# A two-layer graph attention network with a feed-forward block: how the second softmax fetches its 2 x 10,000 logits

## What is computed

```python
as_n = jnp.einsum('nhd,hd->nh', h, a_src)
ad_n = jnp.einsum('nhd,hd->nh', h, a_dst)
e = jax.nn.leaky_relu(as_n[src] + ad_n[dst], NEG_SLOPE)
e_max = jax.lax.stop_gradient(jax.ops.segment_max(e, dst, num_segments=N))
ex = jnp.exp(e - e_max[dst])
denom = jax.ops.segment_sum(ex, dst, num_segments=N)
alpha = ex / (denom[dst] + 1e-16)
```

## Time and profile before

| | |
|---|---|
| median of 3 runs | 4287.79 us (4287.08 to 4290.51) |
| time of the profiled execution | 4294.91 us |
| its span, first to last instruction | 4293.2 us |
| PE busy | 3523.8 us (82%) |
| POOL busy | 1009.2 us (24%) |
| second softmax, first clearing to the store of its records | 3483.73 to 3715.99 us |

### The profile page before, as it was taken

The page is one execution under the profiler, slowest core; times in us unless marked ns, Lnnn a source line. Parts: engine busy times, 40 slices in busy tenths (PEclk is TensorE's granted clock), DMA queues, the critical chain, the costliest instruction groups (busy, mean ns, idle before and its releaser), DMA issues. The chain is left out here.

```text
span 4293.2 us, 67317 instructions
## 1 busy us (share of the span) xinstructions
PE 3523.8 (82%) x21804; PEld 2146.3 (50%) x21805; DVE 2163.2 (50%) x5213; ACT 1302.1 (30%) x2233; POOL 1009.2 (24%) x1392
## 2 busy tenths in 40 slices
PE   4850039999999999999999999999999930188898
PEld 3640025566555655565556555655565520055565
DVE  8877254434443444334434443344334300389998
ACT  2531113322332233223322332233223300044444
POOL 2448710000000000000000000000000037466665
PEclk9985559999999999999999999999999975599999
DMA  8862011111111111111121111111111000278887
GB/s 256 256 211 61 3 38 40 44 56 34 48 40 56 37 46 37 57 38 45 38 56 38 46 40 53 39 48 38 53 39 48 29 13 1 49 213 231 231 230 211
DMA packets 147427, 337.78 MB, mean 79 GB/s; under 512 B 81880, under 2 KB 81880, under 8 KB 139738
## 3 DMA queue, kind: packets, MB, share of 16 engines
q1 hardware_dynamic: 111883, 240.88, 18.4%
q0 software_dynamic: 34112, 93.04, 8.5%
q10 hardware_dynamic: 1175, 0.05, 0.0%
HBM read 266.09 MB, written 124.25 MB: 91 GB/s over the span
## 5 line engine op out<-in xcount | busy, mean ns | idle before, releaser
L942 POOL DMA_INDIRECT lay_rows<-parts,lay_idx x200 | 210.1, 1051 | 2536.2 <-PE lay_pz L1185 1619.2
L1219 PE MATMUL lay_pm<-lay_zh,w1h 128*128 128x500 f16 x1920 | 718.4, 374 | 25.3 <-DVE lay_h L1105 20.1
L1220 PE MATMUL lay_pm<-lay_zl,w1h 128*128 128x500 f16 x1920 | 718.6, 374 | 1.8 <-issue 1.3
L1221 PE MATMUL lay_pm<-lay_zh,w1l 128*128 128x500 f16 x1920 | 718.4, 374 | 0.0
L1026 DVE SCALAR_TENSOR_TENSOR lay_zl<-lay_pz,lay_zh 128x400 f16<-128x400 f32 x600 | 320.4, 574 | 710.7 <-ACT lay_zh L1136 710.5
L1136 ACT ACTIVATE lay_zh<-lay_pz 128x400 f16<-128x400 f32 x600 | 298.3, 504 | 1056.9 <-PE lay_pz L1185 1053.2
L1145 ACT ACTIVATE lay_ex<-lay_pm,b1c,scale 128x500 f32<-128x500 f32 x320 | 245.6, 768 | 869.8 <-PE lay_pm L1221 869.8
L1243 PE MATMUL lay_pm<-w2h,lay_gh 128*128 128x512 f16 x1280 | 484.9, 379 | 0.0
L1243 PE MATMUL lay_pm<-w2h,lay_gl 128*128 128x512 f16 x1280 | 483.9, 378 | 0.0
L1243 PE MATMUL lay_pm<-w2l,lay_gh 128*128 128x512 f16 x1280 | 483.4, 378 | 0.0
L1061 DVE TENSOR_SCALAR lay_ex<-lay_ex,scale 128x500 f32<-128x500 f32 x320 | 153.7, 480 | 568.0 <-ACT lay_ex L1145 568.0
(11 more groups left out here) (278 smaller groups left out, 5775.1 us busy)
## 6 DMA issues: line engine op xcount, KB each, us to landing
x<-in_x_dram SPq DMA_DIRECT2D x20, 1500.0 KB
out_x<-x SPq DMA_DIRECT2D x100, 288.0 KB
out_own<-h SPq DMA_DIRECT2D x100, 288.0 KB
out_dram<-out_x SPq DMA_DIRECT2D x100, 288.0 KB
nrm_xb<-in_x_dram SPq DMA_DIRECT2D x20, 1344.0 KB
parts<-nrm_parts SPq DMA_DIRECT2D x20, 1344.0 KB
h<-lay_h SPq DMA_DIRECT2D x80, 336.0 KB
nrm_w<-in_L_gnn_W_dram SPq DMA_DIRECT2D x6, 1024.0 KB, 19.3
```

Of the source, the lines that this page charges most:

```text
L1219: pe.matmul(o, c.w1h[:, d, cols], zh[:, d, h], start=(d == 0), stop=False)
L1220: pe.matmul(o, c.w1h[:, d, cols], zl[:, d, h], start=False, stop=False)
L1221: ins = pe.matmul(o, c.w1l[:, d, cols], zh[:, d, h], start=False, stop=(d == DC - 1))
```

## The change

The second softmax looks its logits up on chip; the first one stays as it was. A node number is split into its low 7 bits and its high part (0 to 78). The table of 10,000 pairs is loaded once into SBUF as `nodes` (two transfers of SP, from the same `logit2`) and turned by two PE transposes into `tab`: 128 partitions (the low part) by 2 x 79 (the high part). The low parts of the edges are turned the same way into `low_t`.

The 79 columns of edges are worked off in items: 20 items of up to 4 columns for the sources (one value wanted), 27 items of up to 3 columns for the destinations (two values wanted), 47 in all. For an item i of n columns

- *spread* on PE: n f32 matmuls, weights 79 x 128 (a column of the identity, repeated), 128 columns of `low_t` streamed: each of 128 partitions gets a copy of the 128 low parts;
- *apart* on ACT: absolute value of (low part - partition number), 128 x 128n, from PSUM;
- *one* on ACT: relu(1 - that), the one-hot matrix, 128 x 128n;
- *look* on PE: n f32 matmuls, weights 128 x 128 (the one-hot matrix), 79 or 158 columns of `tab` streamed: for each edge the row of the table that has its low part;
- *pick* on DVE: n operations of 128 x 79 or 128 x 158 from PSUM, which keep the entry with the right high part and set the others to zero, and one reduction, which adds them up into `gsrc` or `gdst`.

Tiles between the engines have two buffers. The 158 indirect transfers of this stage are gone; POOL only makes two small ramps (`iota`). What comes behind L685 is unchanged.

```diff
+LOWS = 128
+HIGHS = -(-N // LOWS)
...
+    SIDES = (("src", 1, 4), ("dst", 2, 3))
...
+        self.items = [(side, at, min(group, EC - at)) for side, (_, _, group) in enumerate(self.SIDES)
+                      for at in range(0, EC, group)]
...
+        self.spread = [m.ps(f"spread{b}", [LOWS, 4, EP]) for b in range(2)]
+        self.rows = [m.ps(f"rows{b}", [EP, 512]) for b in range(2)]
...
+    def sync(self, sp):
+        whole, rest = N // LOWS, N % LOWS
+        sp.wait_ge(self.nodes_free, 1)
+        sp.dma_start(self.nodes[0:whole], self.table[0:whole * LOWS, :].rearrange("(p l) h -> p (l h)", l=LOWS))\
+            .then_inc(self.nodes_in, 16)
+        sp.dma_start(self.nodes[whole:whole + 1, 0:rest], self.table[whole * LOWS:N, :].rearrange("(p l) h -> p (l h)", p=1))\
+            .then_inc(self.nodes_in, 16)
+
+    def first(self, dve):
+        self.nc.vector.memset(self.nodes[:], 0.0).then_inc(self.nodes_free, 1)
...
+    def vector(self, dve, ch):
+        nc = self.nc
+        for side, index in enumerate(self.index):
+            ch.put(nc.vector.tensor_scalar(self.cut[:, side, 0], index[:], LOWS - 1, None, ALU.bitwise_and))
+            ch.put(nc.vector.tensor_scalar(self.cut[:, side, 1], index[:], 7, None, ALU.logical_shift_right))
+        ch.wait()
+        nc.vector.tensor_copy(self.cutf[:], self.cut[:]).then_inc(self.cut_ready, 1)
+        dve.wait_ge(self.placed, 2)
+        nc.vector.tensor_copy(self.minus[:], self.place[:]).then_inc(self.highs_ready, 1)
+        ch.put(nc.vector.tensor_copy(self.highs[:], self.highi[:]))
+        dve.wait_ge(self.cut_ready, 1)
+        ch.wait()
+        dve.wait_ge(self.lows_turned, 1)
+        nc.vector.tensor_copy(self.low_t[:], self.spread[0][0:EC, 0:2]).then_inc(self.lows_ready, 1)
+        dve.wait_ge(self.tab_turned, 1)
+        nc.vector.tensor_copy(self.tab[:], self.rows[0][:, 0:2 * HIGHS].rearrange("p (v h) -> p v h", v=2))\
+            .then_inc(self.tab_ready, 1)
+
+        def add(i):
+            side, at, n = self.items[i]
+            values = self.SIDES[side][1]
+            dve.wait_ge(self.picked_ready, i + 1)
+            nc.vector.tensor_reduce(self.found[side][:, at:at + n, 0:values],
+                                    self.picked[:, i % 2, 0:n * values].rearrange("p (c v) h -> p c v h", v=values),
+                                    AX.X, ALU.add).then_inc(self.sums, 1)
+
+        for i, (side, at, n) in enumerate(self.items):
+            values = self.SIDES[side][1]
+            dve.wait_ge(self.rows_done, i + 1)
+            if i >= 2:
+                dve.wait_ge(self.sums, i - 1)
+            for k in range(n):
+                ins = nc.vector.scalar_tensor_tensor(
+                    out=self.picked[:, i % 2, k * values:k * values + values],
+                    in0=self.highs[:].rearrange("p (a h) -> p a h", a=1).broadcast_to([EP, values, HIGHS]),
+                    scalar=self.cutf[:, side, 1, at + k:at + k + 1],
+                    in1=self.rows[i % 2][:, k * values * HIGHS:(k + 1) * values * HIGHS].rearrange("p (v h) -> p v h", h=HIGHS),
+                    op0=ALU.is_equal, op1=ALU.mult)
+            ins.then_inc(self.picked_ready, 1)
+            if i:
+                add(i - 1)
+        add(len(self.items) - 1)
+        dve.wait_ge(self.sums, len(self.items))
+
+    def scalar(self, act):
+        nc = self.nc
+        act.wait_ge(self.highs_ready, 1)
+
+        def one_hot(i):
+            n = self.items[i][2]
+            act.wait_ge(self.apart_ready, i + 1)
+            if i >= 2:
+                act.wait_ge(self.rows_done, i - 1)
+            nc.scalar.activation(self.one[:, i % 2, 0:n], self.apart[:, i % 2, 0:n], ACT.Relu, bias=1.0, scale=-1.0)\
+                .then_inc(self.one_ready, 1)
+
+        for i, (_, _, n) in enumerate(self.items):
+            act.wait_ge(self.spread_done, i + 1)
+            if i >= 2:
+                act.wait_ge(self.one_ready, i - 1)
+            nc.scalar.activation(self.apart[:, i % 2, 0:n], self.spread[i % 2][:, 0:n], ACT.Abs, bias=self.minus[:])\
+                .then_inc(self.apart_ready, 1)
+            if i:
+                one_hot(i - 1)
+        one_hot(len(self.items) - 1)
+
+    def tensor(self, pe):
+        c = self.c
+        pe.wait_ge(self.cut_ready, 1)
+        for side in range(2):
+            ins = pe.transpose(self.spread[0][0:EC, side], self.cutf[:, side, 0], c.ident[0:EP, 0:EP])
+        ins.then_inc(self.lows_turned, 1)
+        pe.wait_ge(self.nodes_in, 32)
+        for v in range(2):
+            ins = pe.transpose(self.rows[0][:, v * HIGHS:v * HIGHS + HIGHS], self.nodes[:, :, v], c.ident[0:HIGHS, 0:HIGHS])
+        ins.then_inc(self.tab_turned, 1)
+        pe.wait_ge(self.lows_ready, 1)
+        pe.wait_ge(self.tab_ready, 1)
+
+        def look(i):
+            side, at, n = self.items[i]
+            width = self.SIDES[side][1] * HIGHS
+            pe.wait_ge(self.one_ready, i + 1)
+            if i >= 2:
+                pe.wait_ge(self.picked_ready, i - 1)
+            for k in range(n):
+                ins = pe.matmul(self.rows[i % 2][:, k * width:k * width + width], self.one[:, i % 2, k],
+                                self.tab[:, 0:self.SIDES[side][1]].rearrange("p v h -> p (v h)"), start=True, stop=True)
+            ins.then_inc(self.rows_done, 1)
+
+        for i, (side, at, n) in enumerate(self.items):
+            if i >= 2:
+                pe.wait_ge(self.apart_ready, i - 1)
+            for k in range(n):
+                ins = pe.matmul(self.spread[i % 2][:, k], c.ident[0:EC, at + k:at + k + 1].broadcast_to([EC, LOWS]),
+                                self.low_t[:, side], start=True, stop=True)
+            ins.then_inc(self.spread_done, 1)
+            if i:
+                look(i - 1)
+        look(len(self.items) - 1)
...
@@ -647,6 +802,9 @@
         def _(pool):
             if more:
                 more.gpsimd(pool)
+            if match:
+                match.gpsimd(pool)
+                return
             pool.wait_ge(loaded, 16 * 9)
             for idx, out, sem in ((src, gsrc, got_src), (dst, gdst, got_dst)):
                 for k in range(EC):
@@ -677,8 +837,11 @@
             ch.put(nc.vector.tensor_scalar(cont[:], first[:], -1.0, 1.0, ALU.mult, ALU.add))
             if more:
                 more.vector(dve)
-            dve.wait_ge(got_src, 16 * EC)
-            dve.wait_ge(got_dst, 16 * EC)
+            if match:
+                match.vector(dve, ch)
+            else:
+                dve.wait_ge(got_src, 16 * EC)
+                dve.wait_ge(got_dst, 16 * EC)
             sides = gsrc[:].rearrange("p c h -> p h c"), gdst[:].rearrange("p c h -> p h c")
@@ -1808,7 +1975,7 @@
             layer_weights(nc, big, c)
             stage_softmax(nc, c, io, dr.logit1, dr.rec1, HEADS, extra=Weights, tag="sm1")
             stage_layers(nc, c, io, dr)
-        stage_softmax(nc, c, io, dr.logit2, dr.rec2, 1, tag="sm2")
+        stage_softmax(nc, c, io, dr.logit2, dr.rec2, 1, matched=True, tag="sm2")
         stage_extra_rows(nc, c, io, dr)
         stage_output(nc, c, io, dr)
 
```

More of the change, by code:

```diff
@@ L586, in vector, with __init__, gpsimd @@
         ch.link(nc.vector.tensor_scalar(c.b1s[:], c.b1[:], c.scale[:, 2:3], None, ALU.mult))
-def stage_softmax(nc, c, io, table, rec, heads, extra=None, tag="sm"):
+LOWS = 128
+HIGHS = -(-N // LOWS)
+class Match:
+    SIDES = (("src", 1, 4), ("dst", 2, 3))
+    def __init__(self, nc, c, m, table, src, dst, gsrc, gdst):
+        self.nc, self.c, self.table = nc, c, table
+        self.index, self.found = (src, dst), (gsrc, gdst)
+        self.items = [(side, at, min(group, EC - at)) for side, (_, _, group) in enumerate(self.SIDES)
+                      for at in range(0, EC, group)]
+        self.nodes = m.sb("nodes", [HIGHS, LOWS, 2])
+        self.tab = m.sb("tab", [LOWS, 2, HIGHS])
+        self.cut = m.sb("cut", [EP, 2, 2, EC], I32)
+        self.cutf = m.sb("cutf", [EP, 2, 2, EC])
+        self.low_t = m.sb("lows", [EC, 2, EP])
+        self.place, self.minus = m.sb("place", [LOWS, 1], I32), m.sb("minus", [LOWS, 1])
+        self.highi, self.highs = m.sb("highi", [EP, HIGHS], I32), m.sb("highs", [EP, HIGHS])
+        self.apart = m.sb("apart", [LOWS, 2, 4, EP])
+        self.one = m.sb("one", [LOWS, 2, 4, EP])
+        self.picked = m.sb("picked", [EP, 2, 6, HIGHS])
+        self.spread = [m.ps(f"spread{b}", [LOWS, 4, EP]) for b in range(2)]
+        self.rows = [m.ps(f"rows{b}", [EP, 512]) for b in range(2)]
+        names = ("nodes_free", "nodes_in", "placed", "cut_ready", "highs_ready", "lows_turned", "lows_ready", "tab_turned",
+                 "tab_ready", "spread_done", "apart_ready", "one_ready", "rows_done", "picked_ready", "sums")
+        (self.nodes_free, self.nodes_in, self.placed, self.cut_ready, self.highs_ready, self.lows_turned, self.lows_ready,
+         self.tab_turned, self.tab_ready, self.spread_done, self.apart_ready, self.one_ready, self.rows_done,
```

(22 more changed lines are left out.)

## The result

| | median of the runs | change |
|---|---|---|
| before | 4288.27 us (4286.04 to 4291.20, 7 runs) | |
| changed | 4303.18 us (4298.81 to 4310.08, 7 runs) | +14.9 us, ratio 1.0034 [1.0023, 1.0046] |

The kernel became slower, by a third of a per cent. The forecast was 4300 us.

The account below looks back on a forecast made before the run. Bound: a 206 us wait for POOL's 158 indirect transfers. The replacing PE and ACT chain at 1.2 GHz would end 12.3 us later: 4287.8 + 12.3 = 4300 us, own range 4293 to 4314, 8 in 10 range 4264 to 4320.

Parts of the forecast that it names:

- How it is coupled: Lookup loop: PE and ACT take turns despite two buffers, so one item costs the sum of both.
- Rival C: Lookup loop: engines overlap after all and PE alone is the bound; about 60 us off, 4240 us; chance 0.04.
- PE at 1.2 GHz: PE's look and spread in the loop: 3.82 us a source item, 3.27 us a destination item.
- ACT: ACT's apart 0.68 and 0.57 us, one 0.63 and 0.52; the pair 1.21 us (source) and 0.99 us (destination).
- Period: Loop time per item, PE plus ACT's pair plus 0.06 handover: 5.09 us source, 4.32 us destination.
- DVE: DVE's picks and reduction beside the chain: 1.7 and 1.8 us an item, covered by PE's and ACT's chain.
- Before the loop: Preparation before the first spread, which comes at about 3492.5 us; bounds 2 to 5 us.
- Sum: Whole stage: L685 at 3708.4 us where it stood at 3696.09; the change costs 12.3 us.
- The clock is what decides: PE in the loop: clock stays at 1.2 GHz throughout; 2.4 GHz would save 73 us.
- B: Loop clock rises in part, most likely among destination items: 4281 us with 13 of 27 fast, 4261 with all; chance 0.11.
- D: Loop items longer than the bounds, by slower repeated-column weight loads or longer waits: 4319 us; chance 0.10.
- rival A: Loop clock rises early and stays at 2.4 GHz: 4228 us; chance 0.11.

Follow-up runs that it names:

- e1: Changed kernel with ACT's one of item i - 1 put ahead of apart of item i; 4205.68 us, ratio 0.9796 to before.
- e4: Changed kernel with the spread done in f16 in place of f32; 4254.89 us, ratio 0.9910 to before.
- e5: e1 with the spread over all 128 partitions, rows 79 to 127 zero; 4168.86 us, ratio 0.9720 to before.
- e6: Changed kernel, its order kept, with the spread over all 128 partitions, rows 79 to 127 zero; 4237.91 us, ratio 0.9899 to before.
- e2: Changed kernel with 4 unused f32 matmuls on PE between a spread and the next look; 4235.50 us, ratio 0.9863 to before.
- e8: e5 with 33 destination columns looked up on chip and the other 46 gathered by POOL; 4145.24 us, ratio 0.9666 to before.
- e3: Changed kernel with only sources looked up on chip, POOL gathering the 79 destination columns as before; 4189.04 us, ratio 0.9758 to before.

## Why the prediction was right

The sign, the time (4303.18 against 4300, in its own narrow range of 4293 to 4314) and the steps held, by these numbers:

- **How it is coupled.** Held: PE and ACT take turns, and e1 shows by the exchange of two operations that it is the order on ACT that couples them, 1.67 us in each item. Rival C fell.
- **PE at 1.2 GHz.** 3.82 and 3.27 us were worked out for the part of PE. Measured: 3552.30 to 3556.13 is 3.83, and 4.31 less *apart*, *one* and the handover of 0.05 (0.48 + 0.51 + 0.05) is 3.27. The loads with one repeated column took the 333 ns of the earlier trace rows. Loads overlap, so the pace is read from their starts: in e1, 16 f32 records took the 3.41 us of an item, 0.213 us each and two for a call, and in e4 two f16 loads of a burst start 0.11 us apart (3533.55 and 3533.66), one for a call. The Trainium skill ("TensorE: Matmul & The Clock Gate", Part 2) has P / 1.2 ns for a load of P columns, 107 at 128. The f16 loads agree with that; the f32 ones do not, and there the measurement decides. Used for f32, the page's formula would have put the stage some 75 us too low, an estimate.
- **ACT.** *apart* 0.69 and 0.58 (0.68 and 0.57 forecast), *one* 0.62 and 0.51, the pair 1.20. All within 0.01.
- **Period.** 5.08 and 4.31 against 5.09 and 4.32, 17 and 24 times as counted.
- **DVE.** The cover held, but its price was mis-sized: 1.7 and 1.8 us were worked out, and it is 3554.34 to 3555.65, 1.31, and 1.51 for the destinations (3699.37 to 3700.88, 0.96 + 0.64 with an overlap). I had added whole durations, 4 x 0.29; four picks in a row took 0.92, 0.21 from one start to the next. It cost the forecast nothing, since DVE is not on the path of the changed kernel, but in e5 it is.
- **Before the loop.** The first spread came 3486.27 - 3483.79 = 2.5 us behind L677's last operation (L837 now), as forecast (3489.7 + 2.5, and 0.3 for the clearing).
- **Sum.** 12.1 us in the stage against 12.3. In the medians it is 14.9, with an interval of 0.23% to 0.46%, 10 to 20 us.
- **The clock is what decides.** Right in both halves, for a reason that was only partly right. It stayed at 0.50, rivals A and B didn't come (nor did D, with both periods within 0.01 us), and where it does rise the period is what I had worked out: 3.35 and 2.82 against 3.4 and 2.9, 65 to 68 us off (e6, e2) against 73. But I argued from PE's busy share and the gap. e6 kept the gap and had the high clock; e1 had no gap and kept the low one for 63 us. What separates e6 from the changed kernel is that in the latter 79 of 128 partitions took part in half of the loop's matmuls. That isn't all of it: in the last 41 us of e1 the spreads still used 79 and the clock was 1.00, and what else counts stays open. The forecast rested on the earlier trace rows and took the loop to be like their first stretch, but they show like busy shares at either level (3.34 of 4 us at 0.50, 3.05 at 1.00), and I never asked what streams in them. So the level was forecast rightly with some luck: rival A was 49 rows of zeros away.

The Trainium skill, in "TensorE: Matmul & The Clock Gate", Part 1, says that "activity releases the throttle", and under "Why this matters for your kernels" it advises to keep TensorE busy without a break. e2 agrees with the rule, and so does the clock of 1.00 in e5; e1 does not as the advice is put, with PE busy in 63 of 63 us at 0.50. Part 2, under "LDWEIGHTS", says that the partitions in use don't matter for the time of a load, and in that the trace agrees (333 ns with 79, 329 with 128, both at 0.50).

Where did the expected gain go? Not to contention and not off the path: 206 us of waiting for gathers were taken out and a chain of 218 us was put in their place, in which the three engines that now work are busy 161 (PE), 50 (ACT) and 70 us (DVE) of 224. Of the 144 us that e8 finds, the clock (e6) is worth some 65 of the changed kernel's time, the order (from e6 to e5) 69, and the gathers beside it 24; with the 15 us of the change itself, 65 + 69 + 24 - 15 = 143. The shares of clock and order hang on which is taken first, since each saves more where the other is still bad: the other way round the order is worth 98 us (changed kernel to e1) and the partitions 37 (e1 to e5).

## What to carry to other kernels

When one resource's chain is replaced by another's, cost the new chain as a cycle: follow which instruction of which engine stands behind which wait, and see whether two buffers really let the engines overlap, or an operation of item i behind one of item i + 1 makes them take turns. Read the granted clock of a matmul loop before its instruction count; if it is low though PE is busy, look at how many partitions the operands fill, and try zeros. And where the old resource is free, keep a share of the work on it.

## What was not expected of the hardware

- The same loop, instruction for instruction, ran at a granted clock of 0.50 with 79 partitions in its spreads and, after its first items, at 1.00 with 128, of which 49 held zeros: 224.4 against 154.2 us for the stage (changed kernel, e6). With the other order on ACT it was 125.0 against 92.7 (e1, e5), and there the loop of 79 partitions rose to 1.00 too, but only among the destination items.
- PE busy for 63 of 63 us ran at 0.50 (e1); PE busy for 12.23 of 20 us, with 1.29 us of nothing in each 3.35, ran at 1.00 (e6).
- Indirect transfers kept their pace of 1.30 us beside PE busy in 14.82 of 20 us (e3), and beside PE busy in 20.00, DVE in 16.86 and ACT in 14.88 of 20 us (e8), and in e3 PE kept its period of 5.08 beside them.
- Four DVE operations in a row from PSUM, 0.29 us each, took 0.92 us together: each started 0.21 us behind the one ahead, before that had ended.
